# A token model with attention and experts on one core: the turn's queues reordered, weighings ahead of gates, an idle load in the drain

## The chip, the core and the metric

The kernel runs on 1 core of a Trainium2 chip. The metric is the device time of one execution in microseconds. TensorE (PE) multiplies matrices into PSUM banks; VectorE (DVE), ScalarE (ACT) and GpSimd (POOL) work on the rest; SyncE (SP) issues nearly all transfers. Each engine works off its own queue in the order in which the program was written, and waits on semaphores.

## The reference, cut to what matters

Input are 32 rows of 512 tokens (a skill id of 75 and a right/wrong bit). Everything is float32.

```
h = where(valid, concat(skill*w+b, attempts*w+b, mastery*w+b) @ proj.T + proj_b, 0)   # 64 wide
# attention, a recurrence over the 512 positions, v = layernorm(h):
x_t   = 0.97 * x_{t-1} + relu(v_t @ Dx.T);  x_t /= max(sum|x_t|, 1e-12)                 # 256 wide
a_t   = rho_{t-1} @ x_t;  y_t = relu(ln(a_t) @ Dy.T) * relu(x_t);  out_t = ln(y_t @ E.T)
rho_t = 0.97 * rho_{t-1} + ln(v_t) x_t^T
h = h + out
# experts: the top 2 of 8, softmax of their logits, all experts computed densely
xn = layernorm(layernorm(h)) * gamma + beta;  logits = xn @ Wr + br
h = h + sum_e w_e * (gelu(xn @ W1[e] + b1[e]) @ W2[e] + b2[e])
```

`attempts` and `mastery` are running counts per row and skill. The output is 32 x 512 x 64.

## The kernel before, in words

A first part (to about 137 us) counts, embeds and prepares weights. Then come 32 turns, one for each row of 512 tokens ("batch"), written for each engine in its function `turn(i, ...)`; turns 4 to 29 are a hardware loop of two turns a pass, the others are written out. A turn is a pipeline: in turn i the attention of batch i, the residual and norm of batch r = i-1, the router of t = i-2, the experts of k = i-3 and the output of i-4 are at work. Last comes `drain()` for the experts of batches a = 29, b = 30 and c = 31.

The order in each queue is written by hand. No planner sets it. The attention works in four chunks of 128 tokens. In TensorE's order: `scores(i, 0..3)` multiplies the scanned states of chunk with chunk (line 1431), with `hidden(k, e)` (two 512-column matmuls, 1549 and 1550) in between; `state_of`, `expert_out(k, q)` (1561), `values`, `y_core` (1492), `hidden(k, 4)`, the router's `weights_T`, `hidden(k, 5)`, `attn_var`, the next batch's `update` 0 and 1 (1420), `hidden(k, 6)`, `fold` (two transposes, 1577), `hidden(k, 7)`, `z_out` (1512), `expert_out` 2 and 3, `z_rows` (1521).

`hidden(e)` may start when Gelu e-2 is done (one of two PSUM banks is free). `scores(3)` needs `diagonal(i, 1)`, since both use one bank. `update(i+1, 0)` needs the first two gate instructions, `update(i+1, 1)` all four (`wait(pe, dv_y, 2 * NK * b + NK * (k - 1))`), since they write the banks that `y_core` filled.

VectorE: `diagonal` masks the scores (1037), `residual` adds the normed attention to h (four instructions, 1068; needs GpSimd's `z_scaling`), then the router of t: `logit_sum` (1073), `logit_bias` (1078), `largest`, `which` (its first instruction gives `gap`), `one_hot`, `softmax` (1101, needs ScalarE's `tanh`), `place` (1106), `merge` (1115, fills `w_flat`); `weigh(k, q)` (two instructions, 1124) multiplies an expert output by rows of weights and needs `expert_out(k, q)`; `gate` (1053, needs `y_core`), `z_eps`, the input and scan of the next batch (1022, 1031), `finish`.

ScalarE: `off_diagonal`, `gelu` (634), `tanh` (639), `h_square` (four squares, 665), `attn_T` (613), `centred_high` (622, x_p<-xc), `weights_T` (645, wT<-bank). GpSimd: `z_scaling` (442), `add_pairs` (469), `add_halves` (473), `add_experts` (479) for the expert sums, `h_scale` (450, a power) after the squares, `xc` (453), `centred_input`, `centred_low`, `mean_back` and `weighted_input`. SP: `spread(t)` stores wT in DRAM (337) and loads it back as rows for all 128 partitions (341), because `weigh` needs them so; `spread_last` (346, 352) does it for batch 31.

## Time and profile before

| what | value |
|---|---|
| median of 3 runs | 693.77 us (692.97 to 695.46) |
| profiled execution | 694.66 us, span 692.9 us, mean TensorE clock 0.995 of full |
| busy in the span | PE 637.5 us (92%), DVE 548.6 (79%), ACT 435.2 (63%), POOL 341.2 (49%) |
| DMA | 60.41 MB, mean 87 GB/s |
| chain that ended last | PE 72%, DVE 11%, ACT 8%, issue 5%, DMA 2% |

From the first `z_rows` (153.6 us) to the last (658.1) the 32 turns are at work; loop turns take alternately 16.46 and 16.43 us. From 658 to 692.9 is the drain. In the rows below a start is in microseconds from the span's start; an arrow names what is written and what is read. Instructions of one engine overlap in a pipeline, so that the sum of durations is longer than the time from start to start.

### The profile page before, as it was taken

To read this page: it belongs to the slowest core of one execution; us is meant where nothing else is said; L and a number is where in the kernel's file an instruction comes from. 1 tells how busy PE (TensorE), PEld (TensorE's weight loads), DVE (VectorE), ACT (ScalarE), POOL (GpSimd) and SP (SyncE) were. 2 spreads that over 40 slices of the span, in tenths; PEclk is the share of its full clock that TensorE was granted. 3 is DMA by queue.
4 is the path that set the end of the run, shared out by engine and by line. 5 is a ranking of instruction groups with operands and counts; after the bars stand their busy time and mean duration, and the time that the engine had idled before them with its cause. 6 is when DMAs were issued, how large, how long until landed. Compare 5 with 4: busy or idle time off the path is not lost.

```text
span 692.9 us, 19220 instructions
## 1 busy us (share of the span) xinstructions
PE 637.5 (92%) x5077; PEld 429.7 (62%) x5077; DVE 548.6 (79%) x1953; ACT 435.2 (63%) x1385; POOL 341.2 (49%) x440
## 2 busy tenths in 40 slices
PE   1582997989999999999999999999999999999997
PEld 0471764456666666666666666666666666666634
DVE  4998888975678888888887888888887888887664
ACT  6990997013566666666666666666666666666682
POOL 2000000933366566555666666655566656655563
PEclk9999999999999999999999999999999999999999
DMA  6200000001434444444444454444444434444454
GB/s 209 105 0 0 2 0 1 12 36 53 94 93 101 100 99 100 99 102 116 110 110 109 108 116 119 102 99 99 99 99 99 99 99 100 100 99 101 93 105 96
DMA packets 61327, 60.41 MB, mean 87 GB/s; under 512 B 21828, under 2 KB 56756, under 8 KB 60788
## 3 DMA queue, kind: packets, MB, share of 16 engines
q1 hardware_dynamic: 58868, 59.34, 35.8%
q10 hardware_dynamic: 2240, 0.73, 0.4%
q8 instruction: 13, 0.21, 0.1%
q14 instruction: 14, 0.11, 0.1%
q0 software_dynamic: 192, 0.01, 0.0%
HBM read 55.18 MB, written 4.89 MB: 87 GB/s over the span
## 4 chain that ended last, share of the span: by engine, by line
PE 72%; DVE 11%; ACT 8%; issue 5%; DMA 2%; ACTq 1%; POOL 0%; SPq 0%; DVEq 0%; POOLq 0%
PE bank L1561 15%; PE bank L1431 13%; PE bank L1549 7%; PE bank L1550 6%; PE bank L1492 5%; PE bank L1512 4%; PE bank L1453 4%; PE bank L1466 3%; ACT skill_rows L634 3%; PE bank L1470 2%; PE bank L1326 2%; PE bank L1442 2%; PE bank L1337 2%; ACT x_p L622 2%; PE bank L1521 2%
## 5 line engine op out<-in xcount | busy, mean ns | idle before, releaser
L634 ACT ACTIVATE skill_rows<-bank,b1T,w_scale 128x512 f32<-128x512 f32 x256 | 194.3, 776 | 57.7 <-PE bank L1550 53.4
L1561 PE MATMUL bank<-skill_rows,w_sb 128*64 128x256 f32 x928 | 116.4, 382 | 0.0
L469 POOL TENSOR_TENSOR feat_parts<-skill_rows 128x512 f32<-128x512 f32 x62 | 78.9, 1272 | 73.5 <-DVE feat_parts L1031 67.8
L1431 PE MATMUL bank<-feat_parts 128*128 128x256 f32 (+1 forms) x512 | 104.2, 337 | 1.9 <-DVE feat_parts L1031 0.9
L1561 PEld LDWEIGHTS bank<-skill_rows,w_sb 128*64 128x64 f32 x928 | 63.1, 137 | 37.4 <-issue 11.0
L1431 PEld LDWEIGHTS bank<-feat_parts 128*128 128x128 f32 x512 | 77.3, 190 | 12.4 <-DVE feat_parts L1037 6.2
L1053 DVE SCALAR_TENSOR_TENSOR feat_parts<-bank,feat_parts 128x256 f32<-128x256 f32 x128 | 45.3, 417 | 46.2 <-PE bank L1492 46.2
L1031 DVE TENSOR_TENSOR_SCAN feat_parts<-same,feat_parts 128x512 f32<-128x512 f32 x62 | 74.3, 1237 | 0.0
L657 ACT ACTIVATE bank<-bank 128x64 f32<-128x64 f32 x128 | 26.6, 220 | 50.9 <-PE bank L1521 50.9
L597 ACT ACTIVATE feat_parts<-bank 128x128 f32<-128x128 f32 x64 | 17.6, 275 | 61.2 <-DVE feat_parts L1037 61.2
L1124 DVE SCALAR_TENSOR_TENSOR skill_rows<-bank,b2T,skill_rows 128x256 f32<-128x256 f32 x120 | 50.8, 473 | 3.6 <-PE bank L1561 2.5
L1068 DVE SCALAR_TENSOR_TENSOR h_all<-bank,z_scaling,h_all 128x64 f32 (+1 forms) x128 | 27.5, 277 | 30.6 <-POOL z_scaling L442 30.6
L1124 DVE SCALAR_TENSOR_TENSOR skill_rows<-bank,b2T,feat_parts 128x256 f32<-128x256 f32 x112 | 47.4, 473 | 1.3
L1549 PE MATMUL bank<-xT_even,w1k 128*128 128x512 f16 x120 | 45.8, 382 | 1.4 <-ACT skill_rows L634 0.5
L447 POOL TENSOR_TENSOR h_var<-h_sq,eps_sq 128x4 f32<-128x4 f32 x32 | 6.4, 201 | 81.2 <-ACT h_squares L665 81.2
L1550 PE MATMUL bank<-xT_even,w1k 128*128 128x512 f16 x120 | 45.5, 379 | 0.0
L1549 PE MATMUL bank<-xT_odd,w1k 128*128 128x512 f16 x112 | 42.8, 382 | 0.9
L1550 PE MATMUL bank<-xT_odd,w1k 128*128 128x512 f16 x112 | 42.5, 379 | 0.0
L473 POOL TENSOR_TENSOR feat_parts<-feat_parts 128x512 f32<-128x512 f32 x31 | 39.3, 1267 | 2.4
L1022 DVE SCALAR_TENSOR_TENSOR feat_parts<-bank,same 128x512 f32<-128x512 f32 x62 | 39.6, 678 | 0.0
L1037 DVE TENSOR_TENSOR feat_parts<-bank,mask_sb 128x128 f32<-128x128 f32 x128 | 35.5, 277 | 4.0 <-PE bank L1431 3.8
L1492 PE MATMUL bank<-aT,dyT 64*128 64x256 f32 x256 | 36.3, 402 | 0.0
(278 smaller groups left out, 1494.7 us busy)
## 6 DMA issues: line engine op xcount, KB each, us to landing
skill_rows<-w_d SPq DMA_DIRECT2D x32, 512.0 KB, 6.1
same<-factor_d SPq DMA_DIRECT2D x31, 512.0 KB, 5.2
feat_parts<-w_d SPq DMA_DIRECT2D x30, 512.0 KB, 6.1
skill_rows<-skill_row_d SPq DMA_DIRECT2D x4, 1024.0 KB, 8.0
out<-o_sb SPq DMA_DIRECT2D x28, 128.0 KB, 4.9
feat_parts<-w_d SPq DMA_DIRECT2D x4, 256.0 KB, 4.9
w_sb<-in_L_ffn_W ACTq DMA_DIRECT2D x2, 256.0 KB
w_d<-wT SPq DMA_DIRECT2D x32, 16.0 KB, 1.4
```

The costliest lines, as they stand in the source:

```text
L469: pool.tensor_tensor(half[:, n, :], tm[:, 2 * n, :], tm[:, 2 * n + 1, :], ALU.add).then_inc(po_half, 1)
L473: pool.tensor_tensor(acc.rearrange("p two t -> p (two t)"), half[:, 0, :], half[:, 1, :], ALU.add)\
L634: act.activation(hid[:, e, :], banks[e % len(banks)][:, :], ACT.Gelu, bias=b1T[:, e:e + 1], scale=w1_scale[:, e:e + 1]).then_inc(ac_gelu, 1)
L1022: dve.scalar_tensor_tensor(relu_b[:, k, :], n_bank[k][:, :], 0.0, factor[:, 1, :], ALU.max, ALU.mult)\
L1031: dve.tensor_tensor_scan(xs[:, k, :], factor[:, 0, :], relu_b[:, k, :], 0.0, ALU.mult, ALU.add)\
L1053: dve.scalar_tensor_tensor(of_half(ys[:, k], half), core[:, k], 0.0, of_half(xs[:, k], half), ALU.max, ALU.mult).then_inc(dv_y, 1)
L1124: last = dve.scalar_tensor_tensor(tm[:, q, cols], z_bank[q % 2][:, cols], b2T[:, e:e + 1], wb[side][:, e, :], ALU.add, ALU.mult)
L1431: last = pe.matmul(n_bank[sc % 2][:, 0:SPAN[sc]], xs[:, k, sc * P:(sc + 1) * P], xs[:, k, sc * P:sc * P + SPAN[sc]], start=(k == 0), stop= ...
L1492: last = pe.matmul(n_bank[half][:, k * 2 * P:(k + 1) * 2 * P], dyT[rows, k * P:(k + 1) * P], aT[rows, :], start=True, stop=True)
L1549: pe.matmul(h_bank[e % 2][:, :], w1k[:, 0, e, :], xT[side][:], start=True, stop=False)
L1550: pe.matmul(h_bank[e % 2][:, :], w1k[:, 1, e, :], xT[side][:], start=False, stop=True).then_inc(pe_hid, 1)
L1561: last = pe.matmul(z_bank[q % 2][n * D:(n + 1) * D, at:at + S // 2], w2_sb[:, e, :], hid[:, e, n * (S // 2):(n + 1) * (S // 2)], start=Tru ...
```

## The change

On VectorE `diagonal(i, 1)` goes ahead of `residual`, and `weigh(k, 1)` ahead of the two gates. On ScalarE `h_square` goes ahead of `tanh`, and `centred_high` ahead of Gelu 4. On GpSimd `weighted_input` goes ahead of `mean_back`. On TensorE `hidden(k, 6)` goes between the two updates. In the drain the weight transposes of batch 30, the logits of batch 31, the folds and one `finish` move; the wait for VectorE's weighings of batch 29 goes from ScalarE to SP; and SP issues a small load (128 x 16 numbers of the masks into a part of `pm` that is no longer used) which nobody waits for before the last store.

VectorE's queue in the second turn of the loop, around `residual` (`h_all<-bank,z_scaling,h_all`; the masked `feat_parts<-bank,mask_sb` are `diagonal`), before:

```order
L1037 TENSOR_TENSOR feat_parts<-bank,mask_sb 128x128
L1068 ISA
L1068 SCALAR_TENSOR_TENSOR h_all<-bank,z_scaling,h_all 128x64
L1068 ISA
L1068 SCALAR_TENSOR_TENSOR h_all<-bank,z_scaling,h_all 128x64
L1068 ISA
L1068 SCALAR_TENSOR_TENSOR h_all<-bank,z_scaling,h_all 128x64
L1068 ISA
L1068 SCALAR_TENSOR_TENSOR h_all<-bank,z_scaling,h_all 128x64
L1035 REGISTER_ALU
L1037 TENSOR_TENSOR feat_parts<-bank,mask_sb 128x128
L1073 TENSOR_REDUCE lg<-bank 128x32
```

The same place after:

```order
L1049 TENSOR_TENSOR feat_parts<-bank,mask_sb 128x128
L1047 REGISTER_ALU
L1049 TENSOR_TENSOR feat_parts<-bank,mask_sb 128x128
L1080 ISA
L1080 SCALAR_TENSOR_TENSOR h_all<-bank,z_scaling,h_all 128x64
L1080 ISA
L1080 SCALAR_TENSOR_TENSOR h_all<-bank,z_scaling,h_all 128x64
L1080 ISA
L1080 SCALAR_TENSOR_TENSOR h_all<-bank,z_scaling,h_all 128x64
L1080 ISA
L1080 SCALAR_TENSOR_TENSOR h_all<-bank,z_scaling,h_all 128x64
L1085 TENSOR_REDUCE lg<-bank 128x32
```

The second masked chunk has moved from behind the four instructions to ahead of them, so that the logit sum follows the residual directly.

ScalarE's queue in turn 30, from the copy of the state (`state<-bank`) on; `skill_rows<-bank,b1T,w_scale` is a Gelu. Before:

```order
L608 ACTIVATE state<-bank 128x128
L634 ACTIVATE skill_rows<-bank,b1T,w_scale 128x512
L639 ACTIVATE tanh_g<-gap 128x4
L665 ACTIVATE h_squares,h_sq<-h_all 128x64 x4
L613 ACTIVATE aT<-bank 128x256
L617 ACTIVATE a_sq<-bank 128x256
L634 ACTIVATE skill_rows<-bank,b1T,w_scale 128x512
L622 ACTIVATE x_p<-xc 128x4x64
L645 ACTIVATE wT<-bank 32x128
L634 ACTIVATE skill_rows<-bank,b1T,w_scale 128x512 x3
```

After:

```order
L618 ACTIVATE state<-bank 128x128
L644 ACTIVATE skill_rows<-bank,b1T,w_scale 128x512
L676 ACTIVATE h_squares,h_sq<-h_all 128x64 x4
L649 ACTIVATE tanh_g<-gap 128x4
L623 ACTIVATE aT<-bank 128x256
L627 ACTIVATE a_sq<-bank 128x256
L632 ACTIVATE x_p<-xc 128x4x64
L644 ACTIVATE skill_rows<-bank,b1T,w_scale 128x512
L656 ACTIVATE wT<-bank 32x128
L644 ACTIVATE skill_rows<-bank,b1T,w_scale 128x512 x3
```

The tanh stands behind the squares, and the copy of xc ahead of the fifth Gelu instead of behind it.

VectorE's queue in turn 30, from `merge` on; `skill_rows<-bank,b2T,skill_rows` is a weighing, `feat_parts<-bank,feat_parts` a gate. Before:

```order
L1115 TENSOR_TENSOR w_flat<-pick 128x4x8
L1119 ISA
L1120 REGISTER_ALU
L74 ISA
L1124 SCALAR_TENSOR_TENSOR skill_rows<-bank,b2T,skill_rows 128x256 x2
L1053 SCALAR_TENSOR_TENSOR feat_parts<-bank,feat_parts 128x2x128 x2
L1053 SCALAR_TENSOR_TENSOR feat_parts<-bank,feat_parts 128x256 x2
L1119 REGISTER_ALU
L1124 SCALAR_TENSOR_TENSOR skill_rows<-bank,b2T,skill_rows 128x256 x2
```

After:

```order
L1127 TENSOR_TENSOR w_flat<-pick 128x4x8
L1131 ISA
L1132 REGISTER_ALU
L74 ISA
L1136 SCALAR_TENSOR_TENSOR skill_rows<-bank,b2T,skill_rows 128x256 x2
L1131 REGISTER_ALU
L1136 SCALAR_TENSOR_TENSOR skill_rows<-bank,b2T,skill_rows 128x256 x2
L1065 SCALAR_TENSOR_TENSOR feat_parts<-bank,feat_parts 128x2x128 x2
L1065 SCALAR_TENSOR_TENSOR feat_parts<-bank,feat_parts 128x256 x2
```

The four gate instructions now follow two weighings instead of one.

The diff, cut to its core:

```diff
 # SP
+            def keep_rings_running(gaps):
+                sp.wait_ge(dv_gap, gaps)
+                sp.dma_start(idle_rows, masks[:, 0:16]).then_inc(ld_idle, 16)
 ...
             def spread_last(side):
                 sp.wait_ge(ac_wT, B)
                 sp.dma_start(w_d[side].rearrange("e (c p) -> (e c) p", c=C), wT[:]).then_inc(st_w, 16)
+                sp.wait_ge(dv_tm, NP * (B - 2))
                 sp.wait_ge(st_w, 16 * B)
 ...
             turn(B - 1, True, True, True, False, 1)
+            keep_rings_running(B - 1)
             spread(B - 2, 0)
 # GpSimd, turn
                 if res:
                     centred_low(i - 1)
-                    mean_back(i - 1)
                 if ahead:
                     weighted_input(i + 1)
+                if res:
+                    mean_back(i - 1)
 # ScalarE, weights_T, turn, drain
-                wait(act, dv_tm, NP * (b - 1))
+                if not isinstance(b, int) or b < B - 1:
+                    wait(act, dv_tm, NP * (b - 1))
 ...
+                if res:
+                    h_square(r)
                 if rt:
                     tanh(t)
-                if res:
-                    h_square(r)
                 if att:
                     attn_T(i)
                     attn_square(i)
+                if res:
+                    centred_high(r)
                 if mlp:
                     gelu(k, 4)
-                if res:
-                    centred_high(r)
                 if rt:
                     weights_T(t)
 ...
-                for e in range(3, 6):
+                for e in range(3, 5):
                     gelu(a, e, drain_h)
+                weights_T(b)
+                gelu(a, 5, drain_h)
                 centred_high(c)
-                weights_T(b)
 # VectorE, drain, turn
-                for q in range(NP):
+                for q in range(NP - 1):
                     drain_weigh(c, q)
                 drain_finish(b)
+                drain_weigh(c, NP - 1)
                 last_finish()
 ...
                     diagonal(i, 0)
+                    diagonal(i, 1)
                 if res:
                     residual(r)
-                if att:
-                    diagonal(i, 1)
 ...
                     weigh(k, 0, 1 - side)
+                    weigh(k, 1, 1 - side)
                 if att:
                     gate(i, 0)
                     gate(i, 1)
-                if mlp:
-                    weigh(k, 1, 1 - side)
-                if att:
                     z_eps(i)
 # TensorE, drain, turn
+                weights_T(b)
                 drain_out(a, 1)
-                weights_T(b)
 ...
+                logits(c, 1)
                 drain_out(a, 3)
-                logits(c, 1)
 ...
                 drain_out(c, 0)
+                drain_fold(a)
                 drain_hidden(c, 6)
                 drain_hidden(c, 7)
-                drain_fold(a)
                 drain_out(c, 1)
+                drain_out(c, 2)
                 for e in range(2):
                     last_fold(0, e)
-                drain_out(c, 2)
-                for e in range(2):
-                    last_fold(1, e)
+                drain_fold(b)
                 drain_out(c, 3)
-                drain_fold(b)
-                for q in range(2, NP):
+                for q in range(1, NP):
 ...
                     update(i + 1, 0)
-                    update(i + 1, 1)
                 if mlp:
                     hidden(k, 6, 1 - side)
+                if ahead:
+                    update(i + 1, 1)
```

## Rows read from the trace of the kernel before

**Rows 1.** One loop turn: busy time of each engine, clock, DMA.

```profile
394.96:411.42 16.46, 16.40 (x134) 11.22 (x132) 13.48 (x48) 10.72 (x35) 9.94 (x14) 1.00 0.46 106
```

**Rows 2.** TensorE in time: start, us, what, how many, idle before.

```profile
396.91 0.61 PE L1431 MATMUL bank<-feat_parts 128*128 128x128 f32 x4
...
397.90 1.63 PE L1431 MATMUL bank<-feat_parts 128*128 128x256 f32 x8
...
406.54 0.62 PE L1420 MATMUL bank<-feat_k,table_k 128*128 x2
407.00 0.38 PE L1549 MATMUL bank<-xT_odd,w1k 128*128 128x512 f16 x1
...
407.43 0.38 PE L1577 MATMUL bank<-ident_f,both 128*128 128x128 f32 x2
407.87 0.39 PE L1549 MATMUL bank<-xT_odd,w1k 128*128 128x512 f16 x1
```

**Rows 3.** TensorE in turn 30, the scores of chunks 2 and 3.

```profile
628.12 1.55 PE L1431 MATMUL bank<-feat_parts 128*128 128x256 f32 x8
```

**Rows 4.** VectorE in the turn at 394.96.

```profile
397.71 0.86 DVE L1068 SCALAR_TENSOR_TENSOR h_all<-bank,z_scaling,h_all 128x64 f32 x4 [1.00 <-POOL z_scaling L442]
398.48 0.28 DVE L1037 TENSOR_TENSOR feat_parts<-bank,mask_sb 128x128 f32<-128x128 f32 x1
...
398.96 1.19 DVE L1078 TENSOR_TENSOR lg<-lg,br_sb 128x32 f32<-128x32 f32 x1
...
402.29 0.17 DVE L1101 TENSOR_SCALAR wgt<-tanh_g 128x4 f32<-128x4 f32 x1 [0.47 <-ACT tanh_g L639]
...
403.14 0.88 DVE L1124 SCALAR_TENSOR_TENSOR skill_rows<-bank,b2T,feat_parts 128x256 f32<-128x256 f32 x2
405.29 1.42 DVE L1053 SCALAR_TENSOR_TENSOR feat_parts<-bank,feat_parts 128x256 f32<-128x256 f32 x4 [1.27 <-PE bank L1492]
```

**Rows 5.** ScalarE in the same turn.

```profile
402.05 0.22 ACT L639 ACTIVATE tanh_g<-gap 128x4 f32<-128x4 f32 x1
402.14 0.27 ACT L665 ACTIVATE h_squares<-h_all 128x64 f32 x1
...
402.38 0.26 ACT L665 ACTIVATE h_squares<-h_all 128x64 f32 x1
...
405.92 0.78 ACT L634 ACTIVATE skill_rows<-bank,b1T,w_scale 128x512 f32<-128x512 f32 x1 [1.80 <-PE bank L1550]
406.59 0.41 ACT L622 ACTIVATE x_p<-xc 128x256 f16<-128x256 f32 x1
406.90 0.25 ACT L645 ACTIVATE wT<-bank 32x128 f32<-32x128 f32 x1
407.06 2.23 ACT L634 ACTIVATE skill_rows<-bank,b1T,w_scale 128x512 f32<-128x512 f32 x3
```

**Rows 6.** GpSimd in the same turn.

```profile
398.84 1.26 POOL L473 TENSOR_TENSOR feat_parts<-feat_parts 128x512 f32<-128x512 f32 x1
...
403.63 1.02 POOL L450 TENSOR_TENSOR h_scale<-h_var,power 128x4 f32<-128x4 f32 x1
```

**Rows 7.** All engines in turn 30, the logit bias and GpSimd's sum.

```profile
629.04 0.19 DVE L1078 TENSOR_TENSOR lg<-lg,br_sb 128x32 f32<-128x32 f32 x1
629.07 1.29 POOL L473 TENSOR_TENSOR feat_parts<-feat_parts 128x512 f32<-128x512 f32 x1
```

**Rows 8.** All engines in the drain, the merge and GpSimd's power.

```profile
663.14 1.09 POOL L450 TENSOR_TENSOR h_scale<-h_var,power 128x4 f32<-128x4 f32 x1
663.39 0.22 DVE L1115 TENSOR_TENSOR w_flat<-pick 128x32 f32<-128x32 f32 x1
```

**Rows 9.** The chain that ended last, in order of time: start, us, what.

```profile
665.61 3.70 DMA w_d<-wT
```

**Rows 10.** TensorE in the drain.

```profile
678.16 1.08 PE L1608 MATMUL bank<-skill_rows,w_sb 128*64 128x256 f32 x8 [1.38 <-DVE skill_rows L1139]
```

**Rows 11.** The page's DMA issues: how often, KB each, median us to landing.

```profile
w_d<-wT SPq DMA_DIRECT2D x32, 16.0 KB, 1.4
```

More of the change, by code:

```diff
@@ L196, in program @@
         last_tm = over(parts_flat, 2 * S, NP, S)
+        idle_rows = pm[:, 0:16]
         last_o = [over(parts_flat, n * C * D, C, D) for n in range(4)]
@@ L201, in program @@
         ld_w3 = sem("ld_w3")
-        ld_wb_late = sem("ld_wb_late")
+        ld_wb_late, ld_idle = sem("ld_wb_late"), sem("ld_idle")
         ld_rows = [sem(f"ld_rows{n}") for n in range(4)]
@@ L375, in _ @@
                 store(B - 4 + n, last_o[n])
+            sp.wait_ge(ld_idle, 16)
             sp.wait_ge(st_out, 16 * B)
```

## The prediction

> **What bounds the kernel.** I read the busy times by stretch first. A loop turn lasts 16.46 us and TensorE is busy for 16.40 of them at full clock, VectorE 13.48, ScalarE 10.72 [rows 1]. So a turn is TensorE's queue, and what another engine costs is seen only as a hole between TensorE's matmuls. "Busy" hides such holes, since a matmul's row is longer than its place in the queue: I looked for them in TensorE's timeline, from start to start. Two matmuls of 512 columns start 0.43 us before what follows them (407.00 to 407.43 [rows 2]), 0.215 each. Two holes lie in places that the change touches.
>
> First, the eight matmuls of `scores` 2 and 3 take 1.63 us in a loop turn [rows 2] and 1.55 in turn 30 [rows 3]. The last four need `diagonal(i, 1)`, which VectorE does after `residual`, at 398.48 [rows 4]. Price of being late: 0.08 us.
>
> Second, `hidden(7)` starts at 407.87, 0.44 us after the fold at 407.43 [rows 2]; the fold's row is 0.38 long like that of one 512-column matmul, whose place is 0.215, so I give it 0.22. It waits for the sixth Gelu, the first of the three that ScalarE starts at 407.06 [rows 5], three in 2.23, about 0.76 each: it ends at 407.82. From `update(0)` to `hidden(7)` are 1.33 us (406.54 to 407.87); the queue alone needs 0.215 + 0.43 + 0.215 + 0.22 = 1.08. Price: 0.25 us.
>
> Outside the 32 turns the drain counts: TensorE stands idle there for 1.38 us behind VectorE, which waits for the weight rows of batch 30 [rows 10].
>
> **The turn, part by part.** All times are those of the turn at 394.96.
>
> *diagonal(i, 1) ahead of residual.* `residual` starts at 397.71 after 1.00 us of idling for `z_scaling` [rows 4], and the scores for `diagonal(i, 1)` end at about 397.52 (396.91 + 0.61 [rows 2]). It fits in, but not wholly: it holds VectorE from about 397.56 for 0.20 (as each of the four instructions of `residual` that make up 0.86), so `residual` moves to 397.76, 0.05 later, and in turns of the other parity perhaps 0.09. TensorE's first hole closes: -0.08.
>
> Behind it `logit_bias` would start at 398.96 - 0.20 + 0.05 = 398.81. Today it starts at 398.96, 0.12 behind GpSimd's `add_halves` (398.84 [rows 6]), and takes 1.19 instead of the 0.19 of turn 30, where it starts 0.03 ahead of the same operation (629.04 against 629.07 [rows 7]). Its end, 400.15, is 0.05 behind that of the GpSimd operation (398.84 + 1.26). So the two exclude each other and the first in has its way. New: 398.81 against 398.84. I take it that VectorE is first, as in turn 30; the other way is priced below. Then `diagonal(i, 2)` and ScalarE's `off_diagonal(2)`, which waits for it, come a microsecond earlier; the next Gelus are then bound by TensorE alone, and the fourth ends its issue at about 401.85 instead of 402.05.
>
> *h_square ahead of tanh.* A square takes 0.24 (402.14 to 402.38 [rows 5]), four 0.96. They start at 401.85, 0.29 earlier than now; `tanh` starts at 402.81 instead of 402.05, 0.76 later. The softmax follows `tanh` by 0.24 (402.05 to 402.29), the first weighing follows by 0.85 (403.14 [rows 4]): 403.05 and 403.90. Behind `tanh` on ScalarE stands `attn_T`, which waits for `values` until after 403.3 anyway: nothing.
>
> *weigh(1) ahead of the gates.* One weighing is two instructions of 0.48, issued 0.40 apart (0.88 for both [rows 4]). Two weighings run from 403.90 to 405.50, `expert_out(1)` having ended at about 404.2. The gates start at 405.29 today, released by `y_core` [rows 4]; now at about 405.52. The four end after 1.42, at 406.94. `update(i+1, 0)` needs the first two (406.28), `update(i+1, 1)` all four. TensorE is ready for the first at 406.54 - 0.08 = 406.46: it doesn't wait. The second now stands behind `hidden(6)`, at 406.46 + 0.215 + 0.43 = 407.11: 0.12 of slack. In the old order (slot 406.68) the late gates would have cost 0.3, so this edit is worth nothing alone and carries the other. The scans come 0.5 us earlier, since a weighing (0.80) left their front; `scores` of the next turn had slack there already.
>
> *centred_high ahead of gelu(4).* The squares 0.29 earlier bring GpSimd's `xc` to about 405.2, so the copy runs 405.26 to 405.57 in time that ScalarE spends idle before `gelu(4)` (405.92, released by TensorE [rows 5]; 405.84 now, as TensorE is 0.08 ahead). Today the copy stands between the fifth and the sixth Gelu and takes 0.31 of issue (406.59 to 406.90, where `weights_T` starts). The sixth Gelu starts at 407.06 - 0.08 - 0.31 = 406.67 and ends at 407.43. `hidden(7)` has its slot at 407.11 + 0.215 + 0.22 = 407.55: no hole. -0.25.
>
> *weighted_input ahead of mean_back* on GpSimd: both are over before the scans in either order, nobody waits; nothing.
>
> Per turn 0.32 to 0.33, that is 16.12 instead of 16.44. Over 26 loop turns -8.4. Turn 30 has no first hole (-0.24), turn 31 has both `hidden(6)` and `hidden(7)` behind Gelus and gains the copy's 0.31, turn 3 counts as a loop turn (-0.3). Turns 0 to 2 are not bound by TensorE's queue: I count 0.1 for `diagonal(i, 1)`. Sum of the turns: -9.35.
>
> **The drain.** *Weight transposes earlier.* ScalarE's copy for batch 30 stood behind the Gelu 5 and the x copy; the store left at 665.61 [rows 9]. Now it stands behind Gelu 4 and leaves at about 664.4. The chain row shows 3.70 us for that store of 16 KB [rows 9]; then the rows are loaded. With all of it 1.2 earlier VectorE can weigh at 675.9, and TensorE's 1.38 us [rows 10] is nearly gone, even if the store stays slow. *The idle load* touches no data that anybody waits for before the last store. Its price lies between nothing and one store's 3.70 on the same queue; since it is let go by `dv_gap`, which VectorE gives before `merge` (663.39 [rows 8]), a microsecond or two ahead of the store, I take nothing. What it may give: the store takes 1.4 us at its median over the 32 [rows 11], so at most 2.3; the stall that this would shorten is gone by then. *TensorE's order:* `weights_T(b)` ahead of `drain_out(a, 1)` must wait for `merge` (663.39 + 0.22 [rows 8]) and a copy earlier `logits(c)` waits for xT: together I count +0.6 of new holes. *The last folds:* three stretches of transposes together instead of two behind waits on weighings: I take 0.1 for each wait saved; -0.2. *The wait moved from ScalarE to SP* brings the last store forward by some 0.3, behind the loads of batch 30: nothing. Sum of the drain: -1.38 + 0.6 - 0.2 = -1.0, with ends of -2.5 and +1.0.
>
> **The sum.** The profiled execution took 694.66 us, span 692.9 and 1.8 around it. 694.66 - 9.35 - 1.0 = 684.3. The median of the runs, 693.77, lies 0.9 below the profiled one; from it the same sum gives 683.4. I say 684.0.
>
> **Rivals.**
> *GpSimd first.* The margin of 0.03 us may fall the other way. Then `off_diagonal(2)` and the three Gelus stay where they are, the squares start at 402.05, `tanh` at 403.00, the gates at 405.70 and end at 407.12. `update(0)` waits 0.05 (406.51), `update(1)` hardly more, and a turn gains 0.26: 26 turns give 6.8, the rest 2.0, 685.4 from the mean of both bases. For it: all 26 loop turns lose today, by 0.08 to 0.12. Against: the edit moves it by more than that.
> *Half of it comes back.* The copy no longer delays `hidden(7)`, but `hidden(6)`, right behind `update(0)` at 406.68, needs Gelu 4 (405.84 + 0.77 = 406.61), 0.07 of slack, and the gates have 0.12. If both chains are 0.15 later than I have them, a turn gains 0.15 to 0.2: about 688.
> *Late gates, slower than before.* The softmax chain has moved 0.76 later, into GpSimd's power operation `h_scale` (403.63 to 404.65 today [rows 6], 403.3 to 404.4 then). If `place` or `merge` were held off until it ends, as `logit_bias` is by `add_halves`, the first weighing would start at 404.7, the gates at 406.4 and end at 407.8; the second update waits 0.75 and eats all 0.33 and 0.4 more per turn: 27 turns give +11, 705. From 0.46 us of such delay on, the turn is slower than before. Against it: in the drain `merge` ran at 663.39 for 0.22 inside such an operation (663.14, 1.09 long [rows 8]), not held off.
> The Trainium skill, SBUF — State Buffer, section "Who interferes with whom", says that a VectorE instruction with two SBUF inputs contends with any GpSimd instruction that reads SBUF, the second one blocking until the first is over. On `logit_bias` the trace agrees (1.19 beside 0.19). By that rule `merge` too would wait out the power operation and this rival would come; the 0.22 of the row contradicts it, so it gets 4 in 100 and not more.
> *No change.* The holes close but TensorE waits for the same chains elsewhere, such as at `z_out`: for it only that 0.1 us holes before `z_out` and `z_rows` stay as they are. Time 693.
>
> **Chances.** VectorE first 0.48 (684.0, own range 682 to 686), GpSimd first 0.26 (685.4), half back 0.13 (688), no change 0.06, late gates 0.04, other losses such as the drain's 0.03. The range for 8 in 10 is 681 to 689. This kernel's measurement can tell 0.3%, 2.1 us, from no change; faster by more than that 0.87, within it 0.06, slower 0.07.
>
> **What would show it.** The turn: 16.1 us from `z_rows` to `z_rows`. `logit_bias` of 0.2 in the loop (forecast) or 1.2 (GpSimd first). The four matmuls of `scores(3)` right behind the others, 1.55 in all. `hidden(7)` 0.22 behind the fold. The softmax 0.75 later, gates at +10.56 from the turn's start instead of +10.33. In the drain the store for batch 30 a microsecond earlier relative to the turns' end and no idle of TensorE over 0.5 us before `drain_out(b, 3)`. I am wrong if the updates wait for the gates by more than 0.2, if `merge` takes a microsecond, or if the turn stays at 16.4.

## The result, and the profile after

| | before | after |
|---|---|---|
| median | 693.46 us (692.97 to 695.46, 4 runs) | 684.14 us (684.07 to 684.24, 4 runs) |
| profiled execution, span | 694.66, 692.9 | 684.15, 682.4 |
| first to last `z_rows` | 504.5 | 495.5 |
| last `z_rows` to the end | 34.8 | 33.4 |

The ratio is 0.9856, 95% interval 0.9839 to 0.9872: 1.4% faster. TensorE's clock is at full through the loop in both. The changed kernel has a dozen lines more: `diagonal` is line 1049, `residual` 1080, `logit_bias` 1090, `merge` 1127, `weigh` 1136, `gate` 1065 on VectorE; the Gelu 644, tanh 649, squares 676, copy of x_p 632 on ScalarE; `add_halves` 482, `h_scale` 459 on GpSimd; `update` 1430, `hidden` 1559 and 1560, the fold 1587 on TensorE.

One loop turn of after, busy time of TensorE, weight loads, VectorE, ScalarE, GpSimd, then clock, DMA share and GB/s, to be set beside [rows 1]:

```profile
390.31:406.44 16.13, 16.13 (x134) 11.29 (x132) 12.81 (x48) 11.22 (x35) 10.03 (x14) 1.00 0.46 107
```

TensorE has no time left in which it isn't busy: 16.13 of 16.13, against 16.40 of 16.46. Its timeline in that turn (start, us, what, how many), to be set beside [rows 2]:

```profile
393.52 1.55 PE L1441 MATMUL bank<-feat_parts 128*128 128x256 f32 x8
...
402.09 0.38 PE L1430 MATMUL bank<-feat_k,table_k 128*128 x1
402.30 0.38 PE L1559 MATMUL bank<-xT_odd,w1k 128*128 128x512 f16 x1
402.52 0.38 PE L1560 MATMUL bank<-xT_odd,w1k 128*128 128x512 f16 x1
402.74 0.38 PE L1430 MATMUL bank<-feat_k,table_k 128*128 x1
402.95 0.38 PE L1587 MATMUL bank<-ident_f,both 128*128 128x128 f32 x2
403.17 0.38 PE L1559 MATMUL bank<-xT_odd,w1k 128*128 128x512 f16 x1
```

Both holes are gone. The eight matmuls of `scores` 2 and 3 take 1.55 us as in turn 30 [rows 3], and from the first update every start is 0.21 to 0.22 behind the last: `hidden(7)` (403.17) follows the fold by 0.22, where it was 0.44. From `update(0)` to `hidden(7)` are 1.08 us, before 1.33.

VectorE in the same turn (in square brackets its idle time and what ended it), to be set beside [rows 4]:

```profile
394.47 0.19 DVE L1090 TENSOR_TENSOR lg<-lg,br_sb 128x32 f32<-128x32 f32 x1
...
398.67 0.18 DVE L1113 TENSOR_SCALAR wgt<-tanh_g 128x4 f32<-128x4 f32 x1 [1.93 <-ACT tanh_g L649]
...
399.21 0.21 DVE L1127 TENSOR_TENSOR w_flat<-pick 128x32 f32<-128x32 f32 x1
399.52 1.66 DVE L1136 SCALAR_TENSOR_TENSOR skill_rows<-bank,b2T,feat_parts 128x256 f32<-128x256 f32 x4
401.10 1.41 DVE L1065 SCALAR_TENSOR_TENSOR feat_parts<-bank,feat_parts 128x256 f32<-128x256 f32 x4
```

GpSimd beside it [rows 6]:

```profile
394.47 1.33 POOL L482 TENSOR_TENSOR feat_parts<-feat_parts 128x512 f32<-128x512 f32 x1
...
398.97 1.08 POOL L459 TENSOR_TENSOR h_scale<-h_var,power 128x4 f32<-128x4 f32 x1
```

`logit_bias` takes 0.19 instead of 1.19; it and GpSimd's sum are printed with the same start, and VectorE is served first. In 25 of the 26 loop turns it takes 0.19, in the turns of one kind with a lead of 0.025, in the others as here: by the trace's nanoseconds GpSimd starts 1 to 4 ns earlier there, and VectorE is still served first. Turn 4, the first of the loop, is the exception. There GpSimd starts 7 ns earlier, and `logit_bias` waits for it:

```profile
200.77 1.31 DVE L1090 TENSOR_TENSOR lg<-lg,br_sb 128x32 f32<-128x32 f32 x1
```

```profile
200.77 1.27 POOL L482 TENSOR_TENSOR feat_parts<-feat_parts 128x512 f32<-128x512 f32 x1
```

The gates come 0.20 later in that turn than in the others of its kind, `update(0)` 0.10, and the turn lasts 16.23 instead of 16.13. `merge` (399.21) lies inside the power operation (398.97 to 400.05) and takes 0.21; the power operation takes 1.08 there and took 1.02 where nothing of this kind ran beside it [rows 6].

ScalarE in the same turn, beside [rows 5]: the four squares, the tanh, then the copy of x_p ahead of the fifth Gelu (401.46), the weight transposes' copy and the last three Gelus:

```profile
397.49 0.24 ACT L676 ACTIVATE h_squares<-h_all 128x64 f32 x1
...
398.45 0.19 ACT L649 ACTIVATE tanh_g<-gap 128x4 f32<-128x4 f32 x1
...
400.95 0.42 ACT L632 ACTIVATE x_p<-xc 128x256 f16<-128x256 f32 x1 [1.28 <-POOL xc L462]
401.46 0.78 ACT L644 ACTIVATE skill_rows<-bank,b1T,w_scale 128x512 f32<-128x512 f32 x1
402.14 0.25 ACT L656 ACTIVATE wT<-bank 32x128 f32<-32x128 f32 x1
402.30 2.29 ACT L644 ACTIVATE skill_rows<-bank,b1T,w_scale 128x512 f32<-128x512 f32 x3
```

The drain, TensorE:

```profile
654.54 0.33 PE L1579 MATMUL bank<-ident_f,w_flat 128*128 128x128 f32 x1 [0.81 <-DVE w_flat L1127]
...
658.89 0.26 PE L1550 MATMUL bank<-wr_p,xT_odd 128*128 128x24 bf16 x4 [0.26 <-ACT xT_odd L637]
...
667.13 1.95 PE L1618 MATMUL bank<-skill_rows,w_sb 128*64 128x256 f32 x16
```

and SyncE's issues there, in order the idle load, the store of batch 30's weights, its loads, and the store of batch 31's:

```profile
652.91 0.36 SPq L347 DMA_DIRECT2D feat_parts<-in_masks x1
655.21 0.32 SPq L338 DMA_DIRECT2D w_d<-wT x1
656.61 2.22 SPq L342 DMA_DIRECT2D skill_rows<-w_d x2
664.72 0.32 SPq L352 DMA_DIRECT2D w_d<-wT x1
```

The 1.38 us of idling [rows 10] are gone: the sixteen matmuls at 667.13 run through. The loads follow the store by 1.40; before, the store alone took 3.70 [rows 9]. In exchange there are two waits of TensorE, 0.81 for `merge` and 0.26 for xT. Before had one there, for a Gelu:

```profile
663.54 1.08 PE L1608 MATMUL bank<-skill_rows,w_sb 128*64 128x256 f32 x8 [0.70 <-ACT skill_rows L634]
...
675.69 1.08 PE L1608 MATMUL bank<-skill_rows,w_sb 128*64 128x256 f32 x8
```

The matmuls at 675.69 here are those at 667.13 there. Counted from the last `z_rows` (658.05 and 648.94) they start after 17.64 us before and after 18.19 us in the changed kernel: the new waits cost 0.55 net.

### The profile page after: what moved, and what is told of

The parts are those of the page before. It is cut to its first block, busy times and chain, and to the rows that moved or that the text cites. A ratio compares the mean times of both kernels' runs of the same rounds, so it can differ in the third digit from the quotient of the medians.

```text
span 682.4 us, 19223 instructions
## 1 busy us (share of the span) xinstructions
PE 631.3 (93%) x5077; PEld 432.5 (63%) x5077; DVE 530.5 (78%) x1953; ACT 448.7 (66%) x1385; POOL 343.1 (50%) x440
## 4 chain that ended last, share of the span: by engine, by line
PE 84%; DVE 9%; ACT 2%; issue 2%; DMA 1%; SPq 0%; POOL 0%; ACTq 0%; DVEq 0%; POOLq 0%
PE bank L1571 15%; PE bank L1441 13%; PE bank L1559 8%; PE bank L1560 7%; PE bank L1502 5%; PE bank L1522 4%; PE bank L1463 4%; PE bank L1476 3%; PE bank L1452 2%; PE bank L1480 2%; PE bank L1336 2%; PE bank L1298 2%; PE bank L1430 2%; PE bank L1347 2%; PE bank L1327 2%
## 5 line engine op out<-in xcount | busy, mean ns | idle before, releaser
L644 ACT ACTIVATE skill_rows<-bank,b1T,w_scale 128x512 f32<-128x512 f32 x256 | 196.6, 777 | 19.9 <-PE bank L1560 14.0
L1441 PE MATMUL bank<-feat_parts 128*128 128x256 f32 (+1 forms) x512 | 102.2, 333 | 1.4 <-DVE feat_parts L1043 0.9
L1441 PEld LDWEIGHTS bank<-feat_parts 128*128 128x128 f32 x512 | 79.6, 191 | 7.3 <-DVE feat_parts L1043 1.6
L1043 DVE TENSOR_TENSOR_SCAN feat_parts<-same,feat_parts 128x512 f32<-128x512 f32 x62 | 72.2, 1205 | 0.0
L1113 DVE TENSOR_SCALAR wgt<-tanh_g 128x4 f32<-128x4 f32 x32 | 5.6, 176 | 57.5 <-ACT tanh_g L649 57.5
L1034 DVE SCALAR_TENSOR_TENSOR feat_parts<-bank,same 128x512 f32<-128x512 f32 x62 | 41.3, 688 | 0.3
L632 ACT ACTIVATE x_p<-xc 128x256 f16<-128x256 f32 x32 | 13.3, 417 | 39.1 <-POOL xc L462 39.1
```

Source lines behind the costliest of these rows:

```text
L644: act.activation(hid[:, e, :], banks[e % len(banks)][:, :], ACT.Gelu, bias=b1T[:, e:e + 1], scale=w1_scale[:, e:e + 1]).then_inc(ac_gelu, 1)
L1034: dve.scalar_tensor_tensor(relu_b[:, k, :], n_bank[k][:, :], 0.0, factor[:, 1, :], ALU.max, ALU.mult)\
L1043: dve.tensor_tensor_scan(xs[:, k, :], factor[:, 0, :], relu_b[:, k, :], 0.0, ALU.mult, ALU.add)\
L1441: last = pe.matmul(n_bank[sc % 2][:, 0:SPAN[sc]], xs[:, k, sc * P:(sc + 1) * P], xs[:, k, sc * P:sc * P + SPAN[sc]], start=(k == 0), stop= ...
```

## The experiments

The first four ran beside before at 693.65 us, the next four beside 694.19, the last four beside 694.73. Distances "behind `z_rows`" are counted from the second of its two transposes (390.47 in the turn shown above, the first being at 390.31). "Turn" is the mean distance from `z_rows` to `z_rows` over the 26 loop turns: 16.445 before, 16.137 after (turn 4 lasts 16.23, for the reason above, the others 16.133).

### Turn alone, drain alone, idle load

e2_turn_only: the changed turn with the drain of before, without the idle load.

> The kernel before with all edits of the turn and none of the drain. Forecast terms: the turns give 9.0 to 9.35, the drain's 1.4 is missing: 685.3 to 685.8, period of a loop turn 16.13, and TensorE's idle time of about 1.4 us in the drain is there as before. Rival: the drain's stall goes by the turns' new order alone: 684.1.

Measured: 684.99 us, ratio 0.9864 (0.9842 to 0.9886); turn 16.137, drain 34.34. That is 0.3 under the range I had given.

e3_drain_only: the drain of after (idle load included) with the turn of before.

> The changed kernel with the turn of before: the drain edits and the idle load alone. By the terms of the forecast 692.0 to 692.8, loop turns of 16.46 and 16.43 us. Rival (the drain edits give nothing by themselves): 693.5.

Measured: 693.84 us, ratio 0.9997 (0.9985 to 1.0008); turn 16.454, drain 33.43. I had expected 692.0 to 692.8; the rival, that the drain's edits give nothing by themselves, is what the times show.

The turn carries the gain. The drain's 1.39 us are seen in the profiles, not in the times: there it is worth nothing that can be told (the low end of its interval, 0.9985, is 1.0 us; the loop turns of this profile are 0.009 longer than those of before, 0.2 us in all). e2_turn_only and the changed kernel (0.9864 and 0.9856) can't be told apart by their times either. The stall of before may be shorter in executions that were not profiled. It hangs on a store that was slow when it met the loading of instructions (see e10_pe_late_no_idle), and that loading comes anywhere from 8.2 to 14.5 us behind the last `z_rows` in these profiles. No run shows it; this stays open.

e1_no_idle:

```diff
-            keep_rings_running(B - 1)
...
-            sp.wait_ge(ld_idle, 16)
```

> The changed kernel without the idle load and the wait for it. My theory: the store of batch 30's weights gets its slow form back (3.7 us instead of the 1.4 that the changed kernel shows), but VectorE has its weighings of batch 30 at 665.85 and TensorE asks for the first only at about 668.1, so the time stays at 684.1 to 684.6. Rival: the load is what took the drain's stall away, then 685.5 to 686.5. Second rival: the store is 1.4 us long without it too, and nothing changes in the trace.

Measured: 684.12 us against 684.14 with it, ratio 0.9858 (0.9838 to 0.9878); turn 16.133 at the median, drain 33.35. The store takes 1.38 without the idle load too. So the idle load does nothing here, and my expectation that the slow store would come back was wrong.

SyncE in e2_turn_only shows where it did come:

```profile
656.67 0.32 SPq L337 DMA_DIRECT2D w_d<-wT x1
660.20 1.26 SPq L341 DMA_DIRECT2D skill_rows<-w_d x2
```

and TensorE there what it costs:

```profile
668.87 1.08 PE L1606 MATMUL bank<-skill_rows,w_sb 128*64 128x256 f32 x8 [1.05 <-DVE skill_rows L1140]
```

The loads leave 3.53 us behind the store and TensorE stands for 1.05. This is the drain order of before without the idle load, as in before itself.

### Which edits of the turn

e4_two_edits: of the turn's edits only these two, drain as after:

```diff
# VectorE
                     diagonal(i, 0)
+                    diagonal(i, 1)
                 if res:
                     residual(r)
-                if att:
-                    diagonal(i, 1)
# ScalarE
+                if res:
+                    centred_high(r)
                 if mlp:
                     gelu(k, 4)
-                if res:
-                    centred_high(r)
```

> The changed kernel, but in the turn only diagonal(i, 1) ahead of residual and centred_high ahead of Gelu 4; tanh, the second weighing, the updates and mean_back as before. My theory: these two carry the whole gain of a turn, since without the late gates the second update isn't waited for: period 16.13 to 16.15, 684.1 to 684.8. Rival: the weighing ahead of the gates and the split updates give something of their own: period 16.2 or more, 686 or more.

Measured: 684.88 us, ratio 0.9872 (0.9852 to 0.9891); turn 16.153. Two edits give 0.292 of the 0.308 us a turn. All the others together, squares, second weighing, split update, GpSimd, give 0.016.

e5_undo_diag: all of after, with `diagonal(i, 1)` back behind `residual`.

> The changed kernel with diagonal(i, 1) back behind residual. My theory: the hole of 0.08 us between the scores of chunks 2 and 3 returns, logit_bias falls behind add_halves again (1.2 us) and the gates come 0.2 later, which the place of update(i+1, 1) behind hidden(6) just takes up: loop turns of 16.21, 686.2 to 686.6. Rival: the late gates aren't covered and the second update waits as well: 16.3 or more, 688 or more.

Measured: 687.30 us, ratio 0.9896 (0.9878 to 0.9914); turn 16.233, 0.100 above the usual turn of after, and the time lies above the 686.2 to 686.6 that I had expected. VectorE's and then GpSimd's rows:

```profile
396.38 1.20 DVE L1090 TENSOR_TENSOR lg<-lg,br_sb 128x32 f32<-128x32 f32 x1
```

```profile
396.26 1.27 POOL L482 TENSOR_TENSOR feat_parts<-feat_parts 128x512 f32<-128x512 f32 x1
```

GpSimd is 0.12 ahead, and `logit_bias` takes 1.20 again. From start to start on TensorE the first hole is back (`z_rows` to the experts' first product 6.31 us instead of 6.23), and 0.02 more come ahead of `hidden(6)`; in the turns of the other kind the two are 0.045 and 0.055.

e6_undo_copy: all of after, with `centred_high` back behind Gelu 4.

> The changed kernel with centred_high back behind Gelu 4. My theory: hidden(7) waits for Gelu 5 again, 0.24 us a turn: loop turns of 16.37, 690.5 to 691.2. Rival (the gain came from the other edits of the turn, and TensorE would wait elsewhere): below 688.

Measured: 691.29 us, ratio 0.9952 (0.9934 to 0.9970); turn 16.385, +0.25. TensorE there, the fold and `hidden(7)`:

```profile
406.65 0.38 PE L1430 MATMUL bank<-feat_k,table_k 128*128 x1
406.86 0.38 PE L1587 MATMUL bank<-ident_f,both 128*128 128x128 f32 x2
407.32 0.39 PE L1559 MATMUL bank<-xT_odd,w1k 128*128 128x512 f16 x1
```

0.46 from the fold to `hidden(7)` instead of 0.22, the second hole of the forecast back in its place. This edit is the largest: 26 times 0.25 are 6.5 us of the 8.0.

e7_undo_split: all of after, with both updates ahead of `hidden(6)` again.

> The changed kernel with both updates together again, ahead of hidden(6). My theory: the second update is ready 0.26 us before the last gate is done and waits for it: loop turns of 16.39 to 16.40, 691 to 692. Rival: what waits there is hidden behind Gelu 5, on which hidden(7) waits anyway: 16.2, 686.

Measured: 691.43 us, ratio 0.9967 (0.9954 to 0.9981); turn 16.404, +0.27. TensorE there:

```profile
406.40 0.39 PE L1430 MATMUL bank<-feat_k,table_k 128*128 x1 [0.34 <-DVE feat_parts L1065]
406.62 0.38 PE L1559 MATMUL bank<-xT_odd,w1k 128*128 128x512 f16 x1
```

The second update waits for the last gate. In e4_two_edits the updates stand together too and only 0.02 is lost: there the gates start with `y_core`, 10.37 us behind `z_rows` instead of 10.62, because the second weighing stands behind them.

e12_undo_weigh: all of after, with the second weighing back behind the gates.

> The changed kernel with one edit of the turn undone: the second weighing stands behind the gates again. Theory (the turn is worth its 0.32 us by the diagonal, the split update and the copy of x_p alone; where this weighing stands has cover on TensorE either way): loop turns 16.13 to 16.15, 684.1 to 684.7 us. Rival (its place ahead of the gates is what feeds TensorE in time): loop turns 16.2 or longer, 686 us and more.

Measured: 684.75 us, ratio 0.9857 (0.9835 to 0.9879); turn 16.135. VectorE there:

```profile
401.76 1.42 DVE L1065 SCALAR_TENSOR_TENSOR feat_parts<-bank,feat_parts 128x256 f32<-128x256 f32 x4 [0.44 <-PE bank L1504]
```

The gates wait for `y_core` again, 0.26 us earlier in the turn than in after, and it gives nothing: with the split update TensorE comes for them later still. The edit that the change is named after is worth nothing. That it is what costs the 0.27 without the split is read from the gates' start (10.37 here, 10.62 in e7_undo_split, with the squares ahead of the tanh in both); the weighing alone, without the split, was not run.

### Who is first at SBUF

e8_slow_bias was to make `logit_bias` late by a fill (one number in each of 4 partitions, 0.06 us) between `logit_sum` and `logit_bias`.

> The changed kernel with one tiny memset (4 partitions, 1 element) on VectorE between logit_sum and logit_bias in the loop turns, so that logit_bias comes some 0.06 us behind the start of add_halves instead of ahead of it. My theory (the rival GpSimd first, made to happen): logit_bias takes 1.2 us, the softmax comes 0.1 to 0.2 later, loop turns of 16.15 to 16.19, 684.7 to 685.7. Rival: VectorE's delay of a microsecond reaches TensorE in full somewhere: 16.4 or more.

Measured: 685.25 us, ratio 0.9865 (0.9846 to 0.9885); turn 16.137. The fill ran in the time in which `logit_bias` waits for the end of `logit_sum`, and moved nothing: 0.19 in all loop turns but the second. No answer.

e11_gpsimd_first puts a longer fill (64 numbers in each of 4 partitions, 0.11 us) ahead of both:

```diff
                 if rt:
+                    if not isinstance(i, int):
+                        dve.memset(table_c[:], 0.0)
                     logit_sum(t, m)
```

> The changed kernel with a fill of a small table that is not read any more ahead of logit_sum in every loop turn, so that VectorE asks for SBUF after GpSimd at logit_bias. Theory (logit_bias follows GpSimd's add_halves when it is not first: 1.2 us instead of 0.19, and TensorE's next work has cover for part of it, as where the diagonal was put back): loop turns 16.15 to 16.22 instead of 16.133, 684.7 to 686.5 us. Rival (the gates are late by a whole microsecond and the turn goes back to its old length): loop turns 16.4 or longer, 691 us and more.

Measured: 684.81 us, ratio 0.9858 (0.9838 to 0.9879). The median can't be told from that of after. The profile, taken in its slowest execution (687.10; the other three took 684.63 to 684.82, and whether the same happened in them isn't known), tells more than was asked, because the two kinds of turn fell on the two sides. VectorE, two turns one after the other:

```profile
396.74 1.29 DVE L1090 TENSOR_TENSOR lg<-lg,br_sb 128x32 f32<-128x32 f32 x1
```

```profile
412.94 0.19 DVE L1090 TENSOR_TENSOR lg<-lg,br_sb 128x32 f32<-128x32 f32 x1
```

GpSimd's `add_halves` in the same two:

```profile
396.72 1.26 POOL L482 TENSOR_TENSOR feat_parts<-feat_parts 128x512 f32<-128x512 f32 x1
```

```profile
412.95 1.31 POOL L482 TENSOR_TENSOR feat_parts<-feat_parts 128x512 f32<-128x512 f32 x1
```

GpSimd 0.02 ahead: 1.29. VectorE 0.02 ahead: 0.19 (GpSimd's own operation then takes 1.31 instead of 1.26). The first three loop turns have 1.17 to 1.30; from 235 to 607 us this alternates, 1.29 in one kind of turn and 0.19 in the other. The turns with 1.29 last 16.233, the others 16.133. So losing this place costs 0.10 a turn, and TensorE's timeline of such a turn says where:

```profile
404.65 0.38 PE L1561 MATMUL bank<-xT_odd,w1k 128*128 128x512 f16 x1 [0.17 <-DVE feat_parts L1065]
```

This is `hidden(6)`, behind an `update(0)` whose row is missing; the wait is the update's, for the first two gates. They come 0.18 later than in after (10.81 us behind `z_rows` against 10.63), and 0.10 of it is seen. The slack of the first update in after is therefore about 0.09.

### TensorE's order in the drain

e9_pe_late:

```diff
# TensorE, drain
-                weights_T(b)
                 drain_out(a, 1)
+                weights_T(b)
...
-                logits(c, 1)
                 drain_out(a, 3)
+                logits(c, 1)
```

> The changed kernel with TensorE's two steps of the drain, weights_T(b) and logits(c, 1), back in the order of before; VectorE's order and all else as changed. In the profile of the changed kernel TensorE stood 0.81 us at weights_T(b) and 0.64 at logits(c, 1), behind which the output products queue; the row of outputs of row block a came 10.14 us after the last z_rows against 9.40 where TensorE had the old order. Theory (these two idle stretches lie on the path that sets the end): drain 32.7 instead of 33.4, 683.4 us. Rival (the end is set by what the DMAs bring back, or the stall at the last weighing returns): drain 33.4 or longer, 684.1 to 685.

Measured: 684.50 us, ratio 0.9856 (0.9835 to 0.9876); drain 33.43, as in after (33.42). The rival was right. TensorE there:

```profile
654.65 1.08 PE L1618 MATMUL bank<-skill_rows,w_sb 128*64 128x256 f32 x8 [0.70 <-ACT skill_rows L644]
...
657.01 1.08 PE L1618 MATMUL bank<-skill_rows,w_sb 128*64 128x256 f32 x8 [0.59 <-ACT skill_rows L644]
```

The first wait is that of before, for a Gelu. The second is new: ScalarE's copy of the weights now stands ahead of Gelu 5 and needs TensorE's `weights_T`; with that back in its late place, Gelu 5 is late and TensorE waits for it. From start to start, less the place of the matmul ahead (0.215, and 0.31 where the next is an expert's product), the two are 0.77 + 0.66 = 1.43 us, and the two of after 0.98 + 0.42 = 1.40. From 659 on no idle row of TensorE's stands in either. So the old order of one engine does not go with the new order of the other. That the weight store leaves 0.9 us later, counted from the last `z_rows` (7.16 against 6.27), is not seen.

e10_pe_late_no_idle is the same without the idle load.

> As the kernel of e9_pe_late, and without the idle load. Theory (the short store is luck of its moment, the idle load does nothing): store 1.38 us, the same as e9_pe_late within 0.2 us. Rival (a later store after a pause falls into the slow form, 3.5 to 3.7 us instead of 1.38, as in the drain where the turn alone was changed): the weights come 2.2 us later, VectorE stands about 1 us at the last weighing, 684.4 us.

Measured: 684.65 us, ratio 0.9854 (0.9832 to 0.9876); drain 33.38, store 1.38. The idle load doesn't decide, then. The trace points to the moment, in another way than I had it. Counted from the last `z_rows` the store leaves at 7.16 us here and in e9_pe_late, at 7.56 in before and in e2_turn_only, where it was slow, and at 6.27 in the changed kernel. The trace shows what it met there. The packets of before between the store's issue and its landing (665.6 to 669.3):

```profile
q1 hardware_dynamic: 48, 0.02, 2.0%
q8 instruction: 1, 0.02, 1.6%
```

and those of after (655.2 to 656.6):

```profile
q1 hardware_dynamic: 48, 0.02, 4.9%
```

q1 is the queue of the store, q8 one that loads instructions. Its one packet, of 16 KB, is over at 668.21; the last two packets of the store start at 668.20 and 668.26. In e2_turn_only it is the same (659.08; 659.07 and 659.12). In all twelve profiles with the new drain the store had landed before this packet came.

## Why the prediction was right

Forecast 684.0 us, measured 684.14. The terms, all in the profiled execution:

| term | forecast | measured |
|---|---|---|
| up to the first `z_rows` | 0 | -0.13 |
| turns 1 to 3 | -0.4 | -0.60 |
| 26 loop turns | -8.4 | -8.00 |
| turn 30 | -0.24 | -0.25 |
| turn 31 | -0.31 | -0.13 |
| drain | -1.0 | -1.39 |
| sum | -10.35 | -10.50 |

Part of the close hit is luck. Between the medians the gain is 9.3 us, not 10.5: the profiled execution of before is 1.2 us above its median, and executions of before lie up to 2.5 us apart, those of after 0.2. The forecast had taken the middle of two bases, 694.66 and 693.77.

**The two holes** were right in place and price. In the turn at 390.31 the experts' first product comes 0.08 earlier than in the turn at 394.96 before it, and `z_out` 0.33 earlier: 0.08 and 0.25. Putting each edit back brings its hole back (e5_undo_diag, e6_undo_copy).

**The loop** is 0.4 short by the other kind of turn. I worked on one turn and counted it 26 times. In the next one of before the scores show

```profile
414.36 1.60 PE L1431 MATMUL bank<-feat_parts 128*128 128x256 f32 x8
```

not 1.63, so the first hole was 0.05 there and that turn gains 0.30. 13 times 0.03 are 0.4; turn 4, in which GpSimd was first, adds 0.1.

**VectorE first** came true, with a lead of 0.025 in half of the turns (forecast 0.03) and none in the others. The margin was thinner than I argued, since I had looked at one kind of turn, and the rival came in one of the 26: in turn 4 GpSimd is 0.007 ahead. The rival's price was 0.065 a turn against the forecast; it is 0.10. The step that was off is the hand-off from the second gate to the first update. The rival counts 0.05 for it (406.46 to 406.51), which leaves a slack of 0.13 (406.28 to 406.46, less 0.05). In turn 4 of after it is 0.14 (208.34 to 208.48), and the slack is about 0.09.

**Squares, tanh, softmax**: forecast 0.76 later, measured 0.78 for the tanh (7.98 us behind `z_rows` against 7.20) and 0.75 for the softmax. **Gates**: forecast 0.23 later, measured 0.19. The second update's slack, 0.12 in the forecast, is 407.11 less 406.94, 0.17, less 0.05 for the hand-off, which the forecast doesn't say. **Weighing and split**: "worth nothing alone and carries the other", with 0.3 as the price of late gates in the old order; undoing the weighing alone (e12_undo_weigh) changes nothing, undoing the split alone (e7_undo_split) costs 0.27.

**Turn 31**: forecast -0.31, measured -0.13. The Gelus no longer hold TensorE, but the next thing does, which I had not looked for: `hidden(7)` comes 0.30 earlier, but TensorE's transposes of batch 30 behind it give 0.18 back, since they wait until VectorE's `finish` has freed their bank (VectorE, its idle time ended by the fold):

```profile
645.15 0.42 DVE L1056 TENSOR_TENSOR o_sb<-bank,h_all 128x256 f32<-128x256 f32 x1 [0.73 <-PE bank L1587]
```

**The drain**: forecast -1.38 + 0.6 - 0.2, measured -1.39. The new waits cost 0.55 (17.64 to 18.19, above), as forecast. The stall was worth more than its idle row says: from 675.69 to 678.16 are 2.47 us, for eight matmuls that take some 0.9 where nothing holds them (the sixteen at 667.13 have a row of 1.95), so about 1.55 and not 1.38. What is left of the sum, about -0.4, is the folds' new place, for which I took 0.2. I did not pull these last two apart by a run. Against my -1.0 both errors are of one sign. One of my signs failed: TensorE was to stand nowhere for over 0.5 us before `drain_out(b, 3)`, and it stands 0.81 for `merge`.

**Late gates, slower than before** was excluded in the loop as in the drain's row [rows 8]: `merge` runs inside the power operation and takes 0.21. The Trainium skill, SBUF — State Buffer, "Who interferes with whom", would have it blocked for the whole instruction. The trace agrees with that section where the other operation is a sum over 512 elements (1.29 against 0.19, by who is first), and does not where it is a power of 4 elements. Why is not shown by any run.

## What to carry to other kernels

When one engine's queue is the turn, look for holes by distances from start to start, not by idle time, price each from the row of its neighbour that has none, and do it for every kind of turn that alternates. Undo edits one at a time before crediting them: here two moved lines are 95% of the gain in the turn, one edit is worth nothing, and another only pays for it. And an order is a matter of two queues: putting back one engine's alone (e9_pe_late) only moved the wait. Moments of two executions are to be compared from a common event such as the last `z_rows`, not from the span's start: by the span's start the store of e10_pe_late_no_idle seems 0.3 us later than that of e2_turn_only, and it is 0.4 earlier.

## What the hardware showed that I had not expected

- **A race for SBUF is decided by thousandths of a microsecond.** With GpSimd 7 ns ahead `logit_bias` takes 1.31 us (turn 4 of after), with GpSimd 14 to 20 ns ahead 1.29 (e11_gpsimd_first); with GpSimd at most 4 ns ahead (the other turns of after) or VectorE ahead it takes 0.19. At 5 ns it went either way (1.31 in turn 4 of e7_undo_split, 0.19 in turns 8 and 18 of e2_turn_only). VectorE, when second, ends 0.05 behind GpSimd's whole operation. GpSimd, when second, loses far less: 0.06 to 0.07 at a tie (1.32 to 1.33 instead of 1.26), 0.05 with VectorE 0.016 ahead, and nothing with VectorE 0.07 or more ahead, though VectorE's row is 0.19 long. So VectorE holds GpSimd up for less than its own row. Such a margin decides nothing lasting: any edit ahead of it can turn it over.
- **Instruction loading can hold up a small store.** Batch 30's 16 KB store took 3.70 us in before and 3.51 in e2_turn_only, the two profiles with the old drain, and 1.38 or 1.39 in all twelve with the new drain, with or without the idle load. In before, 30 of its 32 packets were over by 1.0 us, and the other two started when the packet that loads instructions ended (q8 above). The same store in other turns tells the same: of the 448 in the 14 profiles, 14 took 2.3 to 4.1 us, among them one of after (224.95, 2.63) and one of e4_two_edits (225.23, 3.54). In 13 of these the last two packets started within 0.02 us of the end of such a packet (16 KB of q8 or 8 KB of q14), in one 0.06 behind it. None of the others took over 1.5 us. The new drain sends the store off 0.4 to 1.3 us earlier, and so it is over first. No run moved the instruction loading by itself. In the drains of before and e2_turn_only batch 31's store (4.09 and 3.66) was also held up by batch 30's loads, which were still running.
- **Two losses in one turn do not add up.** A late `logit_bias` alone costs 0.10 a turn (e11_gpsimd_first); late and with the first hole open, of 0.08 in the one kind of turn, it costs 0.10 as well (e5_undo_diag): TensorE, held up by the hole, comes later to the update that waits for the gates, 0.02 instead of 0.10 us. With GpSimd first, then, closing the first hole would have given nothing.
